# Eigenvectors from factors: sums of squares on ScalarE, the levels' small operations in one array and one scan

## What is computed

```python
deg = jnp.sum(A, axis=0) + jnp.sum(A, axis=1) - jnp.diagonal(A)
d_inv_sqrt = jnp.where(deg > 0, jax.lax.rsqrt(deg), 0.0)
L_norm = d_inv_sqrt[:, None] * (jnp.diag(deg) - A) * d_inv_sqrt[None, :]
_, U = jnp.linalg.eigh(L_norm)
agg = jnp.einsum('mn,bnd->bmd', U.T, features)
```

## Time and profile before

| | us |
|---|---|
| median of 3 runs | 4020.89 (4018.69 to 4020.98) |
| the profiled execution | 4031.49 |
| its span, first to last instruction | 4029.7 |
| VectorE busy in the span | 3082.0 (76%) |
| TensorE busy in the span | 3264.3 (81%) |
| ScalarE busy in the span | 1646.5 (41%) |
| this stage, from the first VectorE instruction (2857.4) to the last (2971.8) | 114.4 |

### The profile page before, as it was taken

One profiled execution on the slowest core, in us unless ns is written; L12 is line 12 of the kernel. 1 busy time (PEld: TensorE's weight loads), 2 busy tenths in 40 slices (PEclk: granted clock), 3 DMA queues, 4 the chain that ended last, 5 costly groups with the idle time before them and its releaser, 6 DMA issues. The chain is left out here.

```text
span 4029.7 us, 66466 instructions
## 1 busy us (share of the span) xinstructions
PE 3264.3 (81%) x16975; PEld 2172.5 (54%) x17214; DVE 3082.0 (76%) x19258; ACT 1646.5 (41%) x6505; POOL 55.6 (1%) x71
## 2 busy tenths in 40 slices
PE   5999999999999999889967667445038999998868
PEld 4777777777777777556633222334014443454356
DVE  7999998888887777998789899999964313555466
ACT  2555554444444444444323322112113315554555
POOL 0000000000000000000000000000000000120000
PEclk9999999999999999997788888555569999999989
DMA  0000000000000000000000000000020000000001
GB/s 11 2 2 2 2 2 1 2 1 2 1 2 1 2 2 2 2 1 1 1 1 1 1 1 1 1 1 1 0 72 0 1 0 0 0 0 0 0 11 32
DMA packets 14175, 16.73 MB, mean 4 GB/s; under 512 B 571, under 2 KB 10214, under 8 KB 13798
## 3 DMA queue, kind: packets, MB, share of 16 engines
q1 hardware_dynamic: 13798, 12.48, 1.1%
HBM read 8.28 MB, written 4.19 MB: 3 GB/s over the span
## 5 line engine op out<-in xcount | busy, mean ns | idle before, releaser
L207 PE MATMUL ps<-zero_stream 128*128 128x512 bf16 x1745 | 549.1, 393 | 6.5 <-issue 0.7
L229 PE MATMUL ps<-vectors,UT 128*128 128x128 f32 x2482 | 392.2, 292 | 0.0
L229 PE MATMUL ps<-vectors,U 128*128 128x128 f32 x2366 | 374.4, 292 | 1.0 <-DVE vectors L505 0.3
L229 PEld LDWEIGHTS ps<-vectors,UT 128*128 128x128 f32 x2482 | 316.4, 193 | 23.4 <-DVE vectors L505 23.4
L229 PEld LDWEIGHTS ps<-vectors,U 128*128 128x128 f32 x2366 | 301.0, 193 | 24.0 <-DVE vectors L505 24.0
L343 ACT ACTIVATE vectors<-WihT,refl 128x4 f32<-128x4 f32 (+2 forms) x383 | 114.9, 300 | 394.7 <-DVE refl L467 394.7
L325 ACT ACTIVATE refl<-ps,tiny 128x1 f32<-128x1 f32 x511 | 133.3, 261 | 292.4 <-PE ps L234 183.6
L207 PEld LDWEIGHTS ps<-zero_stream 128*128 128x128 bf16 x1966 | 214.8, 123 | 56.9 <-issue 23.1
L705 ACT ACTIVATE sturm_signs<-sturm_products,sign_bias 128x576 bf16<-128x576 f32 x96 | 74.4, 775 | 352.5 <-DVE products_mark L732 352.5
L223 PE MATMUL ps<-vectors,ident 128*128 128x22 f32 (+4 forms) x1022 | 192.5, 269 | 20.7 <-DVE vectors L501 20.5
L1688 ACT ACTIVATE gates<-ps,gate_bias 128x512 f32<-128x512 f32 (+1 forms) x252 | 152.5, 636 | 131.0 <-PE ps L1675 95.9
(11 more groups left out here) (613 smaller groups left out, 8342.7 us busy)
## 6 DMA issues: line engine op xcount, KB each, us to landing
out_dram<-x SPq DMA_DIRECT2D x16, 256.0 KB, 2.3
adj<-in_adj_dram SPq DMA_DIRECT2D x1, 1024.0 KB, 5.3
l2w_in<-in_L_gnn_W_dram SPq DMA_DIRECT2D x2, 128.0 KB
Wqkv<-in_L_gnn_Wqkv_dram SPq DMA_DIRECT2D x1, 192.0 KB
L_gnn_W<-in_L_gnn_W_dram SPq DMA_DIRECT2D x2, 64.0 KB
L_gnn_Wg<-in_L_gnn_Wg_dram SPq DMA_DIRECT2D x2, 64.0 KB
x<-in_x_dram SPq DMA_DIRECT2D x4, 0.5 KB
L_gnn_Wo<-in_L_gnn_Wo_dram SPq DMA_DIRECT2D x1, 64.0 KB
```

The lines of the kernel that those rows point to most:

```text
L207: nc.tensor.matmul(psum[t][:],still[:,0:P],still[:],start=False,stop=True,skip_group_check=True)
L229: ins=nc.tensor.matmul(ax(m)[:,o:o+WIDE],A[version(m)%2][:,t,j*P:(j+1)*P],XG[:,t,X_:X_+1].broadcast_to([P,WIDE]),start=t==NT-1,stop=t==b)
```

## The change

The squares and their sums move from VectorE (L1176, L1177) to ScalarE, as four activations with a running sum into `NRM`, behind the copies for levels 1 and 2. The bound from the eigenvalues, and all that depends on `e` and `ind` alone, come ahead of the whole sweeps, for all five levels in one array of 31 columns. What depends on `Zt` is put behind the scans of levels 1 to 3, the Newton step behind those of levels 4 and 5, and there the instruction behind a scan no longer waits for it. The choice of the deciding level, which ran along the levels with remainder and sign, is now seven operations on [128, 4, 6] arrays at the end, one of them a scan over 24 columns. A semaphore (`zt_made`) tells ScalarE when `Zt` is there. Levels lie in the arrays from the last (place 1) to the first (place 5), and place 0 is the first component. The ratio passes and the scans themselves are as before.

```diff
@@ -1082,10 +1082,12 @@
...
-        s4=sb1("vec_small",[P,20,NT]); cz=sb1("cut_z",[P,NT,16]); cv=sb1("cut_v",[P,NT,16]); ind=sb1("block_of_twist",[P,NT,32]); sg=sb1("cut_sign",[P,16]); thr=sb1("deflate_at",[P,1]); lr=sb1("lam_row",[P,N]); lr2=sb1("lam_abs",[P,N])
-        step=sem("vec2_step"); io=sem("vec2_iota"); bc=sem("lam_bc"); sq=sem("norm2_ready"); rt=sem("norm_root"); zt_ready=sem("zt_ready"); zp=sem("z_ps"); hot_ready=sem("twist_ready"); hot_copied=sem("twist_copied"); swept=sem("lane_swept"); cut_swept=sem("cut_swept")
+        s4=sb1("vec_small",[P,20,NT]); cv=sb1("cut_v",[P,NT,32]); cc=sb1("cut_e",[P,NT,32]); ec=sb1("e_at_cuts",[P,32]); six=sb1("levels",[P,8,NT,LANES]); ind=sb1("block_of_twist",[P,NT,32]); sg=sb1("cut_sign",[P,32]); thr=sb1("deflate_at",[P,1]); lr=sb1("lam_row",[P,N]); lr2=sb1("lam_abs",[P,N])
+        step=sem("vec2_step"); io=sem("vec2_iota"); bc=sem("lam_bc"); sq=sem("norm2_ready"); rt=sem("norm_root"); zt_ready=sem("zt_ready"); zp=sem("z_ps"); hot_ready=sem("twist_ready"); hot_copied=sem("twist_copied"); swept=sem("lane_swept"); cut_swept=sem("cut_swept"); zt_made=sem("zt_made")
         sc=lambda j: s4[:,j,:]
         MN,MXP,NRM,Y,R,INV,ZL,RHO,VU,VAL,ACTV,REM,SGN,T0,T1=range(15)
+        ZLS,RHOS,SIGNS,DECIDES,KEEPS,TAKES,CHOSEN,SIZE=(six[:,i] for i in range(8))
+        place=lambda l: LANES-l
         with nc.Block() as block:
...
@@ -1111,7 +1113,10 @@
                 act.wait_ge(hot_ready,NT)
                 twist_of(1); twist_of(2)
-                act.wait_ge(sq,1)
+                act.wait_ge(zt_made,1)
+                for g in range(NT):
+                    nc.scalar.activation(lane[0][:,g],Zt[:,g],ACT.Square,accum_out=s4[:,NRM,g:g+1]).then_inc(sq,1)
+                act.wait_ge(sq,NT)
                 nc.scalar.activation(sc(Y),sc(NRM),ACT.Sqrt).then_inc(rt,1)
                 for l in range(3,LANES): twist_of(l)
...
@@ -1152,73 +1157,93 @@
                 flat=lambda a: a[:].rearrange("p g r -> p (g r)")
-                def sweep_whole():
...
-                sweep_whole()
-                link(nc.vector.tensor_tensor(Zt[:],lane[0][:],lane[1][:],ALU.add))
-                link(nc.vector.tensor_tensor(Zt[:],Zt[:],hot[:],ALU.subtract))
-                link(nc.vector.tensor_tensor(lane[0][:],Zt[:],Zt[:],ALU.mult))
-                nc.vector.tensor_reduce(sc(NRM),lane[0][:],AX.X,ALU.add).then_inc(sq,1)
-                v.wait_ge(sq,1); v.wait_ge(rt,1)
-
-                link(nc.vector.reciprocal(sc(R),sc(Y)))
...
-                k.inc(nc.vector.reciprocal(sc(INV),sc(R)))
+                for l in range(1,LANES):
+                    nb=1<<l-1; h=N>>l
+                    k.inc(nc.vector.tensor_copy(ec[:,nb:2*nb],e[:,h:N:2*h]))
+                v.wait_ge(step,k.at())
+                k.inc(nc.vector.tensor_scalar(sg[:,1:32],ec[:,1:32],0.0,2.0,ALU.is_ge,ALU.mult))
+                link(nc.vector.tensor_tensor(cc[:,:,1:32],ind[:,:,1:32],ec[:,1:32].unsqueeze(1).broadcast_to([P,NT,31]),ALU.mult))
+                k.inc(nc.vector.tensor_scalar(sg[:,1:32],sg[:,1:32],-1.0,None,ALU.add))
+                k.inc(nc.vector.memset(DECIDES,1.0))
+                for l in range(1,LANES):
+                    nb=1<<l-1
+                    k.inc(nc.vector.tensor_reduce(RHOS[:,:,place(l)],cc[:,:,nb:2*nb],AX.X,ALU.add))
                 v.wait_ge(bc,1)
                 link(nc.vector.tensor_scalar(lr[:],psum[0][:],SHIFT,None,ALU.add))
                 link(nc.vector.scalar_tensor_tensor(out=lr2[:],in0=lr[:],scalar=-1.0,in1=lr[:],op0=ALU.mult,op1=ALU.max))
                 link(nc.vector.tensor_reduce(thr[:],lr2[:],AX.X,ALU.max))
                 k.inc(nc.vector.tensor_scalar(thr[:],thr[:],8*2.0**-24/2**0.5,None,ALU.mult))
-                k.inc(nc.vector.memset(sc(REM),1.0)); link(nc.vector.memset(sc(SGN),0.0))
...
+                link(nc.vector.tensor_tensor(Zt[:],lane[0][:],lane[1][:],ALU.add))
+                nc.vector.tensor_tensor(Zt[:],Zt[:],hot[:],ALU.subtract).then_inc(zt_made,1)
+
+                line=lambda a: a[:].rearrange("p g d r -> p (g d r)")
+                ratio_at={}
+                def ratio_to_cut(l):
+                    rat=cut[l-1][:].rearrange("p g d r -> p g (d r)")
+                    link(nc.vector.scalar_tensor_tensor(out=rat,in0=rat,scalar=1.0/PIVOT,in1=ecut[l-1][:].rearrange("p d r -> p (d r)").unsqueeze(1).broadcast_to([P,NT,N]),op0=ALU.min,op1=ALU.mult))
+                    k.inc(nc.vector.tensor_scalar(rat,rat,RATIO_CAP,-RATIO_CAP,ALU.min,ALU.max)); ratio_at[l]=k.at()
+                def sweep_to_cut(l):
+                    v.wait_ge(step,ratio_at[l]); v.wait_ge(hot_copied,l*2*NT)
+                    nc.vector.tensor_tensor_scan(line(swept_cut)[:,::-1],line(cut[l-1])[:,::-1],line(hot_cut[l%2])[:,::-1],0.0,ALU.mult,ALU.add).then_inc(cut_swept,1)
+                def at_cut(l):
+                    v.wait_ge(cut_swept,l)
+                    k.inc(nc.vector.tensor_reduce(ZLS[:,:,place(l)],swept_cut[:].rearrange("p g d r -> p g (d r)")[:,:,0::N>>l],AX.X,ALU.add))
+                V_=cv[:,:,1:32]
+                ratio_to_cut(1); sweep_to_cut(1)
+                v.wait_ge(zt_made,1)
                 for l in range(1,LANES):
-                    h=N>>l; nb=N//(2*h)
-                    sweep_to_cut(l)
...
-                    k.inc(nc.vector.tensor_reduce(sc(ZL),swept_cut[:].rearrange("p g d r -> p g (d r)")[:,:,0::h],AX.X,ALU.add))
...
-                    k.inc(nc.vector.tensor_tensor(sc(SGN),sc(SGN),sc(T1),ALU.add))
-                    link(nc.vector.tensor_tensor(sc(REM),sc(REM),sc(ACTV),ALU.subtract))
-
-                link(nc.vector.tensor_scalar(sc(T1),Zt[:,:,0],0.0,-2.0,ALU.is_gt,ALU.mult))
...
-                link(nc.vector.tensor_tensor(sc(INV),sc(INV),sc(SGN),ALU.mult))
+                    nb=1<<l-1; h=N>>l
+                    k.inc(nc.vector.tensor_tensor(cv[:,:,nb:2*nb],Zt[:,:,h:N:2*h],sg[:,nb:2*nb].unsqueeze(1).broadcast_to([P,NT,nb]),ALU.mult))
+                at_cut(1)
+                v.wait_ge(step,k.at())
+                ratio_to_cut(2); sweep_to_cut(2)
+                for l in range(1,LANES):
+                    nb=1<<l-1; h=N>>l
+                    k.inc(nc.vector.tensor_tensor(cv[:,:,nb:2*nb],cv[:,:,nb:2*nb],Zt[:,:,h-1:N:2*h],ALU.add))
+                at_cut(2)
+                v.wait_ge(step,k.at())
+                ratio_to_cut(3); sweep_to_cut(3)
+                link(nc.vector.tensor_tensor(V_,V_,ind[:,:,1:32],ALU.mult))
+                for l in range(1,LANES):
+                    nb=1<<l-1
+                    k.inc(nc.vector.tensor_reduce(SIGNS[:,:,place(l)],cv[:,:,nb:2*nb],AX.X,ALU.add))
+                k.inc(nc.vector.tensor_copy(SIGNS[:,:,0],Zt[:,:,0]))
+                at_cut(3)
+                v.wait_ge(step,k.at())
+                ratio_to_cut(4); sweep_to_cut(4)
+                v.wait_ge(rt,1)
+
+                k.inc(nc.vector.tensor_scalar(SIGNS,SIGNS,0.0,-2.0,ALU.is_gt,ALU.mult))
+                link(nc.vector.reciprocal(sc(R),sc(Y)))
+                k.inc(nc.vector.tensor_scalar(SIGNS,SIGNS,1.0,None,ALU.add))
+                link(nc.vector.tensor_tensor(sc(R),sc(R),sc(NRM),ALU.mult))
+                link(nc.vector.tensor_tensor(sc(R),sc(R),sc(Y),ALU.add))
+                link(nc.vector.tensor_scalar(sc(R),sc(R),0.5,None,ALU.mult))
+                at_cut(4)
+                v.wait_ge(step,k.at())
+                ratio_to_cut(5); sweep_to_cut(5)
+                link(nc.vector.reciprocal(sc(INV),sc(R)))
+                k.inc(nc.vector.tensor_tensor(RHOS[:,:,1:LANES],RHOS[:,:,1:LANES],sc(INV).unsqueeze(2).broadcast_to([P,NT,LANES-1]),ALU.mult))
+                at_cut(5)
+                v.wait_ge(step,k.at())
+                cuts=lambda a: a[:,:,1:LANES]
+                levels=lambda a: a.rearrange("p g l -> p (g l)")
+                link(nc.vector.tensor_tensor(cuts(SIZE),cuts(ZLS),cuts(RHOS),ALU.mult))
+                link(nc.vector.scalar_tensor_tensor(out=cuts(SIZE),in0=cuts(SIZE),scalar=-1.0,in1=cuts(SIZE),op0=ALU.mult,op1=ALU.max))
+                link(nc.vector.tensor_scalar(cuts(DECIDES),cuts(SIZE),thr[:,0:1],None,ALU.is_gt))
+                k.inc(nc.vector.tensor_scalar(KEEPS,DECIDES,-1.0,1.0,ALU.mult,ALU.add))
+                link(nc.vector.tensor_tensor(TAKES,DECIDES,SIGNS,ALU.mult))
+                link(nc.vector.tensor_tensor_scan(levels(CHOSEN),levels(KEEPS),levels(TAKES),0.0,ALU.mult,ALU.add))
+                link(nc.vector.tensor_tensor(sc(INV),sc(INV),CHOSEN[:,:,LANES-1],ALU.mult))
                 for g in range(NT):
                     k.inc(nc.vector.tensor_scalar(Zt[:,g],Zt[:,g],s4[:,INV,g:g+1],None,ALU.mult))
```

More of the change, by code:

```diff
@@ L1173, in _ @@
-                sweep_whole()
-                link(nc.vector.tensor_tensor(Zt[:],lane[0][:],lane[1][:],ALU.add))
-                link(nc.vector.tensor_tensor(Zt[:],Zt[:],hot[:],ALU.subtract))
-                link(nc.vector.tensor_tensor(lane[0][:],Zt[:],Zt[:],ALU.mult))
```

(29 more changed lines are left out.)

## The result

Against the kernel before in the same rounds the changed kernel stands at a ratio of 0.9948, 95% interval 0.9924 to 0.9971 (median 4007.38 us, 3997.75 to 4012.67 in 6 runs; before 4021.33). Two more comparisons of the same kernel, under the experiments, gave 0.9964 (0.9952 to 0.9977) and 0.9966 (0.9952 to 0.9979), or 4006.4 and 4007.2 us, both in the range. So the direction holds, and the question is what in these numbers is the change. One run of the kernel before, 4050.39 us, weighs on the first ratio: by the means of the six runs it is 0.9946, without that run 0.9958, and by the medians 0.9965. One execution of the kernel before under the experiments, 5184.97 us at a granted clock of 0.589, stands in no comparison.

What follows compares the result with a forecast made beforehand. VectorE's in-order chain was taken to bound the stage. Removing 23.17 us, adding 7.63 and saving 0.71 of waits gave 16.2 us less, 4004.7 us from a median of 4020.89; the range was 4001.5 to 4009.5.

Steps and rivals of the forecast that it cites:

- the spread of the runs 2.3: Whole kernel: three runs lay within 2.3 us, which helped set the range's lower end of about 4001.5 us.
- Rival 2: Behind the stage: TensorE's clock rises later, matmuls of 21.51 us take twice as long, 4026.2 us; chance 0.04, slower 0.015.
- reverse case: Behind the stage: TensorE's clock rises some 8 us earlier, giving at most half of 6.44 us, 4001.5; chance 0.045.
- The sum: Changed stage: 23.17 us go, 7.63 come, 0.71 of waits saved; 16.2 us less, stage 98.1 us.
- Before the bound: VectorE ahead of the eigenvalues' bound: copies, sign operations, a product, a memset and five reductions cost 1.58 us.
- Behind the five sweeps: VectorE after each sweep: small products, sums, mask, root operations, reciprocal; reductions at the cuts alone cost 1.33 us.
- The end: VectorE at the stage's end: five waited operations, one unwaited and a short scan cost 1.38 us.
- The scan of 24 columns: VectorE at the stage's end: taken as 0.24 us, between 0.16 and 4.42, with no such scan in the trace.
- All new small operations: VectorE in the stage: 51 new small instructions cost 7.63 us, a short one 0.08 unwaited and 0.20 waited.
- Waits off the path: VectorE: five scans to cuts at 4.34 us for 4.46 save 0.60; the subtraction making Zt, 2.32 to 2.21, saves 0.11.
- ScalarE at nothing: ScalarE in the stage: four squares, at most 3.3 us, and a root, 0.20, stay hidden and cost nothing.
- Rivals 1 and 3: VectorE: 1, unwaited operations cost like waited, 11.7 us less, chance 0.09; 3, new wait before scan 3 or dear short scan, 0.04.

Runs made afterwards that it cites:

- e3: The changed kernel with a wait behind each of the 33 small VectorE operations that had none; the stage took 102.38 us, 4.68 more.
- e2: The changed kernel with the norm's square and sum back on VectorE; the stage took 102.33 us, 4.63 more.
- e5: The changed kernel with GpSimd clamping the ratios of levels 2 to 5, ratio passes one level ahead; the stage took 98.59 us, 0.89 more.

## Why the prediction was wrong at its lower end, and right in its mechanism

**The step that failed** is the range's: downwards it added "the spread of the runs 2.3", and it gave the unchanged part ahead of the stage no term at all. The 2.3 came from three runs. In the rounds of the first comparison alone the kernel before spread over 31.7 us and the changed one over 14.9; over all runs of the study that the comparisons use, the kernel before lies between 4006.05 and 4050.39 us and the changed one between 3995.88 and 4023.28. In the profiled runs the table above says where the spread arose: the tridiagonalisation, ahead of the stage and unchanged, took 1992.4 to 2027.9 us.

Rival 2 looked at TensorE's clock, but only behind the stage; that part moved by 0.91 us between the first two profiles. Its reverse case, an earlier rise, did come in one run, and dearer than the 3.2 us priced: in e3 the part behind took 1051.7 us, 4.9 to 6.3 less than in the other runs. There the clock stood at 1.00 from 8 to 16 us behind the stage, in the other runs at 0.50. The reason stays open.

The hint was there: the profiled execution was 0.26% above the median of the three runs, and the working set that aside. By the stage alone, 16.64 of the 4021.33 us, the ratio is 0.9959, or 4004.2 us. All three intervals hold it; the first comparison's centre lies 4.2 us below, the other two 2.2 and 3.0 above. That the first came out below 4001.5 is most likely the spread, not the change, and that the other two came out inside is in part luck. The medians of the three comparisons lie 12.0 to 14.0 us apart, less than the stage's 16.6, so the whole time can't confirm the stage's gain closer than that.

**The sum** forecast 16.2 us less and a stage of 98.1; measured were 16.64 and 97.70. Term by term:
- Before the bound 1.58 predicted, 1.43 measured (2877.90 to 2879.33).
- Behind the five sweeps, reductions at the cuts included, 4.67 predicted and 4.41 measured (0.70, 0.75, 1.03, 1.25, 0.68).
- The end 1.38 predicted, 1.45 measured. The scan of 24 columns, the term without a row, was 0.24 predicted and 0.25 measured.
- All new small operations: 7.63 predicted, 7.29 measured; a step of 0.08 unwaited was right, and the widths were priced a little high.
- Waits off the path: 4.34 from scan to small operation, as predicted; the subtraction 2.21, as predicted.

**ScalarE at nothing** held: the squares and the root took 2.81 us, against "at most 3.3" and 0.20, and ended some 5 us ahead of sweep 1's end. Rivals 1 and 3 did not come: no idle time ahead of scan 3, no dear short scan, and rival 1's price had to be put in by hand, in e3.

**Where the 16.6 us come from**, by the runs: the norm 4.63 (e2, the 0.10 for the subtraction's wait among it), waits behind small operations at most 4.68 (e3, of which 0.4 are second waits that the kernel before did not have), waits behind five scans 0.62, and the remaining 6.7 or more, which no run isolated. That rest should be 96 small operations becoming 51, and some 0.3 for the wait for the root that is gone. The first and the second were measured one at a time, so that they add up is worked out, not shown.

## What to carry to other kernels

Where one engine runs a chain of small operations in order, put independent ones between the dependent ones and wait once for a group: the wait was 0.13 us a piece here, more than the 0.08 of the operation. Work handed to an idle engine pays in full only if its result is asked for later than it can be ready (4.63 against 2.1 us). GpSimd was no such engine beside VectorE's scans, products and operations with a scalar. For a change of half a per cent read the length of the changed stage in the trace: it repeated within 0.04 us, while the whole time moved by 20 and more, in the profiles with a clock elsewhere.

## What the runs showed that was not expected

- **The granted clock** of the same tridiagonalisation came out at 0.84 to 0.95 from 1500 to 2000 us, in stretches at 1.00 and at 0.50, with TensorE's busy time the same ahead of the fall in the two runs compared.
- **GpSimd and VectorE take turns.** A clamp of 2048 columns took 1.95 us at its shortest and 5.93 beside a scan, and a scan 6.11 for 4.42 beside clamps. This agrees with the Trainium skill's page SBUF — State Buffer (section SBUF: two separate sides): GpSimd shares a pair of ports, as an exclusive lock, with VectorE operations that have two inputs in SBUF or run in a two-port mode, and the side that comes second blocks for a whole instruction. By that rule a clamp beside a scan would wait for its end and then take its 1.95; in e5 it ended 1.68 us after the scan, 0.27 short of that.
